# Routed experts over sorted rows in 40 tiles, in place of sixteen dense experts

## The reference, cut to what matters

```
logits = xf @ Wg                       # xf: 1600 x 128, 16 experts
_, topi = top_k(logits, 2)             # two experts for each token
gates = softmax(logits where chosen, else -inf)
for e in range(16):
    h = silu(xf @ W1[e] + b1[e]) * (xf @ W11[e] + b11[e])     # 128 -> 256
    y = y + (h @ W2[e] + b2[e]) * gates[:, e, None]
z = silu(xf @ Ws1 + bs1) * (xf @ Ws11 + bs11) @ Ws2 + bs2     # shared, 128 -> 512
x = x + y + z
```

## Time and profile before

| | us |
|---|---|
| median of 3 runs | 1759.56 (1759.03 to 1764.13) |
| profiled execution, its time | 1761.54 |
| profiled execution, its span (first to last instruction) | 1759.8 |
| PE busy | 1624.1 (92%) |
| DVE busy | 1256.1 (71%) |
| ACT busy | 981.4 (56%) |
| POOL busy | 978.4 (56%) |

### The profile page before, as it was taken

The page is one execution under the profiler, slowest core; times in us unless marked ns, Lnnn a source line. Parts: engine busy times, 40 slices in busy tenths (PEclk is TensorE's granted clock), DMA queues, the critical chain, the costliest instruction groups (busy, mean ns, idle before and its releaser), DMA issues. The chain is left out here.

```text
span 1759.8 us, 37865 instructions
## 1 busy us (share of the span) xinstructions
PE 1624.1 (92%) x11436; PEld 1563.6 (89%) x11436; DVE 1256.1 (71%) x2678; ACT 981.4 (56%) x1763; POOL 978.4 (56%) x839
## 2 busy tenths in 40 slices
PE   5658999999999999999999999999999957999998
PEld 5547999999999998999899999999999955888887
DVE  4736777767676776777677767777777754888887
ACT  1315656656565655566565656555666533656654
POOL 0027666656565656666575747566565402666665
PEclk9768999999999999999999999999999976999999
DMA  5031110101010111101011111111010011222221
GB/s 88 1 92 45 45 56 28 55 28 50 32 53 29 49 38 44 55 31 54 29 50 32 50 32 49 37 45 55 30 34 28 17 40 68 71 76 83 83 83 38
DMA packets 89712, 83.69 MB, mean 48 GB/s; under 512 B 16003, under 2 KB 87069, under 8 KB 89519
## 3 DMA queue, kind: packets, MB, share of 16 engines
q1 hardware_dynamic: 82816, 79.03, 14.3%
q10 hardware_dynamic: 6703, 2.28, 0.9%
HBM read 77.08 MB, written 4.21 MB: 46 GB/s over the span
## 5 line engine op out<-in xcount | busy, mean ns | idle before, releaser
L961 DVE TENSOR_TENSOR pT_lo<-banks,pT_hi 128x512 fp32r<-128x512 f32 (+1 forms) x672 | 418.4, 630 | 273.4 <-ACT pT_hi L895 267.9
L895 ACT CAST pT_hi<-banks 128x512 fp32r<-128x512 f32 (+1 forms) x672 | 361.5, 543 | 344.6 <-PE banks L1041 338.5
L842 POOL TENSOR_SCALAR probs<-probs,row_inv 128x1448 f32<-128x1448 f32 x192 | 284.7, 1483 | 244.0 <-DVE row_inv L956 243.7
L1041 PE MATMUL banks<-ident,probs 128*128 128x128 f32 x2304 | 365.5, 274 | 10.1 <-POOL probs_half L842 8.0
L1066 PE MATMUL banks<-pT_hi,ctx_hi 128*128 128x256 f32 (+1 forms) x1152 | 355.3, 308 | 13.0 <-DVE pT_lo L961 12.5
L830 POOL TENSOR_SCALAR bias<-mask,c_cur 128x1444 f32<-128x1444 uint8 x192 | 283.6, 1477 | 118.9 <-DVE nmax L949 106.2
L1066 PE MATMUL banks<-pT_hi,ctx_lo 128*128 128x256 f32 (+1 forms) x1152 | 330.6, 287 | 0.0
L1066 PE MATMUL banks<-pT_lo,ctx_hi 128*128 128x256 f32 (+1 forms) x1152 | 329.3, 286 | 0.0
L886 ACT ACTIVATE probs<-probs,nmax 128x1448 f32<-128x1448 f32 x192 | 289.8, 1509 | 36.7 <-DVE nmax L949 36.5
L1041 PEld LDWEIGHTS banks<-ident,probs 128*128 128x128 f32 x2304 | 270.7, 140 | 23.1 <-issue 11.2
L1296 POOL TENSOR_TENSOR gated<-hid,gate_rows 128x400 f32<-128x400 f32 x144 | 172.3, 1202 | 148.4 <-DVE hid L1475 147.3
(11 more groups left out here) (208 smaller groups left out, 2708.2 us busy)
## 6 DMA issues: line engine op xcount, KB each, us to landing
mask<-in_mask_BxSxS_bk SPq DMA_DIRECT2D x192, 180.5 KB
gate_rows<-gates_dram SPq DMA_DIRECT2D x18, 800.0 KB, 4.0
nat<-in_ctx SPq DMA_DIRECT2D x16, 704.0 KB
w_raw<-in_L_ffn_W SPq DMA_DIRECT2D x48, 128.0 KB, 2.1
mask_half<-in_mask_BxSxS_bk SPq DMA_DIRECT2D x16, 90.2 KB
xt<-in_x SPq DMA_DIRECT2D x4, 200.0 KB
x_dram<-xt SPq DMA_DIRECT2D x4, 200.0 KB
n2hi_dram<-n2hi SPq DMA_DIRECT2D x4, 200.0 KB
```

What stands on the lines that cost most here:

```text
L842: pool.tensor_scalar(prob(j)[0:n, :], prob(j)[0:n, :], rinv[0:n, s:s + 1], 1.0, ALU.mult, ALU.mult).then_inc(probs_ready, 1)
L895: act.copy(pT_hi[tslot(i, j)][:, 0:w], banks[:, T_BANK + j % 2, 0:w]).then_inc(turned_hi, 1)
L961: dve.tensor_tensor(pT_lo[tslot(i, j)][:, 0:w], banks[:, T_BANK + j % 2, 0:w], pT_hi[tslot(i, j)][:, 0:w].bitcast(F32), ALU.subtract)\
L1041: last = pe.transpose(banks[:, T_BANK + j % 2, at_col:at_col + 128], prob(t)[:, c0:c0 + 128], ident[:, :])
```

## The change: what it does

Self-attention: POOL also clears a tile of 128 x 40 x 130 elements and writes a spare index in each row; SP stores it to `xs_dram` (2.66 MB) ahead of its x1 stores.

`experts`: POOL copies the normalised rows, so that each token has a row for each of its two experts, with two more columns, the gate and the index 2 x token + k. DVE counts, with two PE products (`places`) by a triangular and an all-ones matrix, the place of each row in its expert's list, rounds each expert's list up to tiles of 128, and gets `pos`. POOL scatters the rows to `xs_dram`, 26 indirect transfers (13 tiles x 2) of up to 128 rows of 520 B. Any distribution of 3200 rows over 16 lists fits in `NSLOT` = 40 tiles; all 40 are always run, filled or not.

While this goes on, the shared expert is computed dense as before, in 16 units (4 chunks x 4 quarters of the width 512), without gates. With each unit the weights of one routed expert are split by ACT and DVE; all stay in SBUF.

Then each of the 40 slots is one tile: PE loads the owner's number from SBUF into a register and uses it in the address of the weights (now the moving operand, 512 columns), adds the bias by a product with a selection matrix that POOL made (`choose`), ACT and DVE form the gated unit, PE turns it, ACT and DVE split it, PE multiplies down, ACT and DVE scale by the gate (128 columns) and POOL scatters the 128 result rows to `yk_dram`. The loop is unrolled; in turn i an engine works on slots i, i-1 and i-2. When all scatters have landed, SP loads both result rows of each token side by side, and DVE adds them to y. The code below is dedented and cut.

```diff
+        sp.wait_ge(empty_made, 3)
+        sp.dma_start(xs_dram.rearrange("(p a) n -> p a n", p=128), empty[:, :, :]).then_inc(xs_zeroed, 16)
...
+        pool.memset(empty[:, :, :], 0.0).then_inc(empty_made, 1)
...
-UNITS = [(m, c) for c in range(NTOK // CT) for m in range(HID // 128)]
+NCH = NTOK // CT
+HT = 2 * HID // 128
+UNITS = [(c, j) for c in range(NCH) for j in range(HT)]
 NU = len(UNITS)
...
+NSLOT = (2 * NTOK + NE * 127) // 128
+XG = NSLOT // 4
+XSLOTS = 3
...
+SELS = 6
+YSLOTS = 4
...
+        for e in range(NE):
+            load(2 + e, W1[e], W11[e], W2[e])
+        sp.wait_ge(scattered, 16 * 2 * TT)
+        for g in range(XG):
+            wait(sp, x_turned, g - XSLOTS + 1)
+            wait(sp, meta_done, 2 * (g - XSLOTS + 1))
+            sp.dma_start(xs[g % XSLOTS], xs_dram[g * 512:(g + 1) * 512, :].rearrange("(t p) n -> p t n", p=128))\
+                .then_inc(xs_in[g % XSLOTS], 16)
+        for i in range(YSLOTS):
+            sp.wait_ge(ys_out[i], 16 * (NSLOT // YSLOTS))
...
+            if g < NTG - 1:
+                sp.dma_start(yk[:, TG[g], :], yk_dram[r0:r1, :].rearrange("(t p k) d -> p t (k d)", p=128, k=2))\
+                    .then_inc(yk_in[g], 16)
...
+        pool.wait_ge(xs_zeroed, 16)
+        pool.wait_ge(rows_copied, NTG)
+        pool.wait_ge(gates_set, 4)
+        pool.wait_ge(pos_set, 1)
+        for t in range(TT):
+            n = 128 if t < TT - 1 else LASTROWS
+            for k in range(2):
+                pool.indirect_dma_start(xs_dram[:, :], bass.IndirectOffsetOnAxis(ap=pos[0:n, k, t:t + 1], axis=0),
+                                        rows[k][0:n, t, :], None).then_inc(scattered, 16)
...
+        def choose(i):
+            wait(pool, down_ready, i - SELS + 1)
+            pool.tensor_copy(sel[i % SELS][:, :], owned[:, i:i + 1].to_broadcast([128, 128]))\
+                .then_inc(sel_ready, 1)
...
+        for i in range(NSLOT):
+            if i % 4 == 0 and i // 4 + 2 < XG:
+                meta(i // 4 + 2)
+            pool.wait_ge(meta_done, 2 * (i // 4 + 1))
+            pool.wait_ge(ys_done, i + 1)
+            pool.indirect_dma_start(yk_dram[:, :], bass.IndirectOffsetOnAxis(ap=id_col[:, i:i + 1], axis=0),
+                                    ys[i % YSLOTS], None).then_inc(ys_out[i % YSLOTS], 16)
+            if i + SELS < NSLOT:
+                choose(i + SELS)
...
+        def split_hi(i, e):
+            act.wait_ge(w_in[i % RAWS], 48 * (i // RAWS + 1))
+            act.copy(up_hi[:, e, :], up_raw[i % RAWS][:, :]).then_inc(hi_done, 1)
+            act.copy(down[:, e, :, 0, :], down_raw[i % RAWS][:, :, :]).then_inc(hi_done, 1)
...
+        for i in range(NSLOT + 2):
+            if i < NSLOT:
+                wait(act, hs_done, i - 1)
+                act.wait_ge(up_ready, i + 1)
+                act.activation(glu[i % 2], bank(2 + i % 2, width=HID), ACT.Silu).then_inc(glu_done, 1)
...
+            if 1 <= i <= NSLOT:
+                k = i - 1
+                act.wait_ge(h_turned, k + 1)
+                wait(act, down_ready, k - 1)
+                act.copy(hT_hi[k % 2], bank(4 + k % 2, width=HID)).then_inc(ht_hi, 1)
+            if i >= 2:
+                k = i - 2
+                act.wait_ge(meta_done, 2 * (k // 4 + 1))
+                act.wait_ge(down_ready, k + 1)
+                wait(act, ys_done, k - 1)
+                act.activation(y_part[k % 2], banks[:, 6 + k % 2, D:2 * D], ACT.Copy,
+                               scale=gate_col[:, k:k + 1]).then_inc(part_done, 1)
...
+        link(dve.tensor_tensor(rank[:, :, :], pick[0][:, :, :], pick[1][:, :, :], ALU.add))
...
+        for n, step in enumerate((2, 4, 8)):
+            a, b = chosen[n % 2], chosen[1 - n % 2]
+            dve.tensor_tensor(b[:, 8:, :], a[:, 8:, :], a[:, 8 - step:8 + TT - step, :], ALU.add)\
+                .then_inc(chosen_done, 1)
+            dve.wait_ge(chosen_done, n + 1)
...
+        dve.wait_ge(rank_ready, 1)
...
+            link(dve.tensor_reduce(pos_f[:, k, :], pick[k][:, :, :], AX.X, ALU.add))
+        dve.tensor_copy(pos[:, :, :], pos_f[:, :, :]).then_inc(pos_set, 1)
+        tall = [128, NSLOT, NE]
+        link(dve.tensor_tensor(reached[:, :, :], ramp[:, :].unsqueeze(2).to_broadcast(tall),
+                               first.unsqueeze(1).to_broadcast(tall), ALU.is_ge))
+        link(dve.tensor_reduce(owner[:, :], reached[:, :, :], AX.X, ALU.add))
+        dve.tensor_scalar(owner_i[:, :], owner[0:1, :], 1.0, None, ALU.subtract).then_inc(owners_set, 1)
+        dve.tensor_scalar(owned[:, :], owner[:, :], part[:, 2:3], None, ALU.is_equal).then_inc(owned_set, 1)
+        dve.wait_ge(b_hi_done, 1)
+        lo = slice(LO_ROW, LO_ROW + NE)
+        dve.tensor_tensor(b_both[lo, :], b_raw[lo, :], b_both[lo, :].bitcast(F32), ALU.subtract)\
+            .then_inc(b_split, 1)
         dve.memset(yT[:, NTOK:TPAD], 0.0).then_inc(out_copied, 1)
...
+        for n in range(NU + 1):
+            if n < NU:
+                c, j = UNITS[n]
+                dve.wait_ge(silu_done, n + 1)
+                wait(dve, hlo_done, n - SLOTS + 1)
+                dve.scalar_tensor_tensor(hid[n % SLOTS][:, :], bank(2 * (n % 2) + 1, width=CT),
+                                         bs_cols[:, 1, j:j + 1], act_out[n % 2][:, :], ALU.add, ALU.mult)\
+                    .then_inc(hid_done, 1)
+            if n:
+                k = (n - 1) % SLOTS
+                dve.wait_ge(hhi_done, n)
+                wait(dve, sh_down, n - SLOTS)
+                dve.tensor_tensor(h_lo[k], hid[k][:, :], h_hi[k].bitcast(F32), ALU.subtract).then_inc(hlo_done, 1)
+            if n < NU:
+                split_lo(2 + n, n)
+            if n % 4 == 3 and n > 4:
+                out_copy(n // 4 - 1)
+        out_copy(NCH - 1)
...
+        for i in range(NSLOT + 2):
+            if i < NSLOT:
+                dve.wait_ge(glu_done, i + 1)
+                wait(dve, h_turned, i - 1)
+                dve.tensor_tensor(hs[i % 2], banks[:, 2 + i % 2, HID:2 * HID], glu[i % 2], ALU.mult)\
+                    .then_inc(hs_done, 1)
...
+            if 1 <= i <= NSLOT:
+                k = i - 1
+                dve.wait_ge(ht_hi, k + 1)
+                dve.tensor_tensor(hT_lo[k % 2], bank(4 + k % 2, width=HID), hT_hi[k % 2].bitcast(F32),
+                                  ALU.subtract).then_inc(ht_lo, 1)
+            if i >= 2:
+                k = i - 2
+                dve.wait_ge(part_done, k + 1)
+                wait(dve, ys_out[k % YSLOTS], 16 * (k // YSLOTS))
+                dve.scalar_tensor_tensor(ys[k % YSLOTS], bank(6 + k % 2, width=D), gate_col[:, k:k + 1],
+                                         y_part[k % 2], ALU.mult, ALU.add).then_inc(ys_done, 1)
         for g in range(NTG):
...
+            dve.wait_ge(yk_in[g], 16)
+            link(dve.tensor_tensor(y[p, ts, :], y[p, ts, :], yk[p, ts, 0:D], ALU.add))
+            dve.tensor_tensor(y[p, ts, :], y[p, ts, :], yk[p, ts, D:2 * D], ALU.add).then_inc(y_added, 1)
...
+        def places():
+            pe.wait_ge(e_consts, NCONST)
+            pe.wait_ge(chosen_done, 3)
+            dst, wide = bank(5, width=TT * NE), "p t e -> p (t e)"
+            pe.matmul(dst, before[:, :], rank[:, :, :].rearrange(wide), start=True, stop=False)
+            pe.matmul(dst, ones[:, :], chosen[1][:, 8:, :].rearrange(wide), start=False, stop=True)
+            pe.matmul(banks[:, 5, 256:256 + NE], ones[:, :], chosen[1][:, 8 + TT - 1, :], start=True, stop=True)\
+                .then_inc(rank_ready, 1)
...
+        def turn_x(g):
+            pe.wait_ge(xs_in[g % XSLOTS], 16 * (g // XSLOTS + 1))
+            wait(pe, x_lo_done, g - 1)
+            for a in range(4):
+                last = pe.transpose(bank(g % 2)[:, a * 128:(a + 1) * 128], xs[g % XSLOTS][:, a, 0:D], ident[:, :])
+            last.then_inc(x_turned, 1)
+        def up(i, e):
+            g, cs = i // 4, slice(i % 4 * 128, i % 4 * 128 + 128)
+            pe.wait_ge(x_lo_done, g + 1)
+            pe.wait_ge(sel_ready, i + 1)
+            wait(pe, hs_done, i - 1)
+            dst = bank(2 + i % 2)
+            w_hi = up_hi[:, bass.ds(e, 1), :].rearrange("p a n -> p (a n)")
+            w_lo = up_lo[:, bass.ds(e, 1), :].rearrange("p a n -> p (a n)")
+            pe.matmul(dst, sel[i % SELS][:, :], b_both[:, 0:2 * HID], start=True, stop=False)
+            pe.matmul(dst, x_hi[g % 2][:, cs], w_hi, start=False, stop=False)
+            pe.matmul(dst, x_hi[g % 2][:, cs], w_lo, start=False, stop=False)
+            pe.matmul(dst, x_lo[g % 2][:, cs], w_hi, start=False, stop=True).then_inc(up_ready, 1)
+        def turn_h(i):
+            pe.wait_ge(hs_done, i + 1)
+            wait(pe, ht_lo, i - 1)
+            for m in range(2):
+                last = pe.transpose(bank(4 + i % 2)[:, m * 128:(m + 1) * 128], hs[i % 2][:, m * 128:(m + 1) * 128],
+                                    ident[:, :])
+            last.then_inc(h_turned, 1)
+        def lower(i, e):
+            pe.wait_ge(ht_lo, i + 1)
```

(89 more changed lines are left out.)

434 lines of the change are left out of this document (214 added, 220 removed).

## The result

The changed kernel takes **1626.3 us** (median of four runs, 1621.8 to 1630.2) beside 1761.8 us for the kernel before in the same comparison: ratio 0.923, 95% interval 0.920 to 0.926. Forecast were 1628 us and a range of 1597 to 1692. The total was right and the way to it was not: slots began 8.6 us later than forecast and then ran 16.3 us shorter. Two later sets measured the same kernel at 1620.1 and 1619.9 us, so it scatters by more than the 2 us that lie between this median and the forecast.

A forecast was written before the change was run, and what follows sets the result against it. It took PE's columns to bound the old kernel; positions at 1468.6, shared part to 1513.0, slots 1514.3 to 1610.3, drain to 1612.8 and the end gave a 1627.9 us span, median 1628 us, range 1597 to 1692.

The forecast's parts named there:

- The bound before: Old expert loop: bound by PE's columns, 1296 products of 400 columns needing 233 of its 279 us.
- Attention part at no cost: Self-attention: POOL's clearing and SP's 2.66 MB store hide under a wait until 92 us; cost 0, at most 13 us.
- Routing added steps: Between logits copy at 1456.2 us and row positions: top-2 chain, then counting and ranking, positions known at 1468.6 us.
- First hid at 1471.6: Start of the shared expert on DVE: 3.0 us of operations after the positions; before the change it was 1475.9.
- Shared units at 2.45 us, bound by DVE: Shared expert with weight splits: 16 units of summed DVE durations, 39.2 us, to 1510.8, finished at 1513.0.
- Stores 1.4 us each, 36.4 in all: POOL's 26 indirect row scatters to slots, from 1468.6 to 1505.0 us; rows loaded by 1510.3, 2.7 before shared part ends.
- Slots at 2.4 us: Forty slots from 1514.3 us: 1.63 of PE array work plus 0.77 of register work each, 96.0 in all.
- Rival (d): Slots: PE's sequencer work is hidden, slots take 1.63 us, 31 us less, total 1597; chance 0.09.
- The end, 15.1 us: After the slots drain at 1612.8: last scatter, landing, gather of 1.6 MB, additions and close, to 1627.9.
- (a): Scatters and slots: POOL's indirect-DMA queue is the bound, governing slots from 1.95 us each; 1690 us at 2.75; chance 0.21.
- (b): Same POOL queue at a losing price, slower than before from 3.8 us each; 1786 us at 4.2; chance 0.05.
- (c): Shared units and slots: PE stays at its lower clock, 1.2 GHz, adding 45 us, 1673 us; chance 0.12.

The follow-up runs named there:

- e6_quiet: Changed kernel with DVE's three subtractions of a shared unit reading one operand from an idle PSUM bank, not SBUF (values wrong); 1614.0 us, ratio 0.915.
- e1_fixed_owner: Changed kernel with each slot's owner a program constant, no register loaded and no operand addressed by one; 1614.9 us, ratio 0.916.
- e2_no_bias: Changed kernel without the first product of each slot (the up bias, 512 columns); 1619.3 us, ratio 0.920.

## Why the prediction was right, step by step

- *The bound before* (PE's columns) and that 128 of 144 units go at so many us each: right.
- *Attention part at no cost*: the clearing of the tile ends at 31.3 us (near 33 was worked out), the transfer takes 8.2 us from issue to landing for 13, and SP's next order comes at 93.2 us for 92.3. So it costs 1 us there at most; what the attentions lost behind it is not told apart from their scatter.
- *Routing added steps*, 12.4 us from logits to positions: 13.2. Right to 0.8 us; 3.4 us of the lateness lie ahead of it, 2.5 of them before the experts begin and the rest up to the logits.
- *First hid at 1471.6*: 1475.9, late by as much as the logits and 0.9 us.
- *Shared units at 2.45 us, bound by DVE*: 2.06 us (first hid 1475.9, last 1506.8). DVE is the busiest and each duration was right (0.63, 0.57, 0.69, 0.42), but they must not be added: the next operation starts about 0.08 us before the one ahead has ended, as 1501.48 to 1501.96 above for one of 0.57. The step added durations where pitches were wanted. 16 units: 6.2 us too many.
- *Stores 1.4 us each, 36.4 in all*: 42.3, from 1473.6 to 1515.9. The price lay between what the prediction named apart: 0.96 + 0.30 alone would be 33 us; the rest is DVE's double reads, which it put at 0.6 us a store and left out of the sum. e6_quiet measured 0.33 a store, 8.6 us. With them the stores end last, by 5 us, and not the shared part. Of the 8.6 us by which the slots begin late, 5.0 are the first store's late start and 5.9 the longer queue, less the 2.7 us that the forecast had as cover; 0.4 us lie in the loading and turning. From the last store's start to SP's load of the slots it is 2.15 us, near the 2.1 taken for the landing. The fixed 2.0 us of the Trainium skill ("DMA: Bandwidth & Descriptors", Anatomy of one DMA) agree with that wait and are no queue time: a store's place in the queue is 1.26 us where DVE is quiet.
- *Slots at 2.4 us*: 1.96. This is the step that failed most. Array work is 1.84 and not 1.63 (e1_fixed_owner). A plain step is 1.71 for 1.57: four up products take 0.97 for 0.90 (the first of a slot takes 0.28, the others keep 0.23), the down part 0.60 for 0.55, two transposes 0.14 for 0.12. Turning new rows adds 0.43 to each fourth step where 0.24 were counted. That 0.06 us a transpose came from a misreading of the earlier trace rows: not four but three transposes lie between 1340.29 and 1340.54 us, 0.11 us from start to start, the third of them

```profile
1340.51 0.27 PE L1041 MATMUL banks<-ident,probs_half 128*128 128x128 f32 x1
```

  The register work is 0.12 and not 0.77: it mostly runs beside the products (e1_fixed_owner, e2_no_bias), so the idle of the rolled loop, from which 0.77 was taken, is no measure of it. Rival (d), hidden, was near the mechanism, and its 1597 us were wrong by the array's 0.21 us x 40, the register work's 0.12 x 40 and the 8.6 us of late start.
- *The end, 15.1 us*: 14.8, from the last slot's result at 1605.17 to 1620.0.
- Together: slots begin 8.6 us late, slots and drain take 82.2 us for 98.5, the end 0.3 less: 1627.9 becomes 1619.9.
- *Rivals.* (a) and (b): a store's place in the queue is 1.63 us ahead of the slots and 1.28 in them, under the 1.95 from which the queue would govern. (c): the granted clock is 0.50 in the gap and 0.97 in the slots; the old loop had 0.99. PE was kept busy in the slots, as the prediction argued. The clock was 0.87 in the shared part, where PE is idle 29% of the time.

That the total is within 2 us of the median is luck: two errors of opposite sign met, slots begun too early and slots priced too dear. Its range held the time for a better reason: the register work and the stores were bounded from both sides.

## What to carry to other kernels

Count a chain on one engine by starts, not by durations, and count the instructions between two starts before dividing. Work that an engine's sequencer does ahead of its array need not be added to the array's: here the larger of the two came nearer than their sum. An indirect store from SBUF was here nearly a fixed price per instruction, and the DVE work beside it, by where it reads from, made a quarter of that price.
